# The feed-forward section's last down product in two halves of columns, each summed by VectorE and sent alone

## The reference

```python
x = x + conv_attention(ln_over_channels(x))      # 7x7 windows, softmax, 64 channels
t = to_tokens(x)                                 # (4, 1024, 64)
h = ln_over_channels_of_tokens(t)
for b in range(33):                              # a scan over 33 blocks, 19 kinds each
    op = argmax(h[0, 0, :19])                    # the kind is read from the data
    y = attention(h, wq[b, op], wk[b, op], wv[b, op], wo[b, op])
    h = where(attn_mask[b, op], y, h)
    z = relu(h @ w1[b, op] + b1[b, op]) @ w2[b, op] + b2[b, op]   # 64 -> 256 -> 64
    h = where(ffn_mask[b, op], z, h)
out = t + h
```

## Time and profile before

| what | us |
|---|---|
| median of 3 runs | 239.64 (239.6 to 239.88) |
| the profiled execution's own time | 239.32 |
| its span in the profile | 237.2 |
| first feed-forward section, first product to last store | 93.4 to 109.7 |
| second one, its last store | 232.3 to 233.0 |
| first and last start of an output transfer's issue | 229.2 and 234.4 |

### The profile page before, as it was taken

One profiled execution on the slowest core, in us unless ns is written; L12 is line 12 of the kernel. 1 busy time (PEld: TensorE's weight loads), 2 busy tenths in 40 slices (PEclk: granted clock), 3 DMA queues, 4 the chain that ended last, 5 costly groups with the idle time before them and its releaser, 6 DMA issues.

```text
span 237.2 us, 5409 instructions
## 1 busy us (share of the span) xinstructions
PE 222.1 (94%) x1995; PEld 153.4 (65%) x1996; DVE 158.4 (67%) x294; ACT 156.1 (66%) x304; POOL 26.2 (11%) x37
## 2 busy tenths in 40 slices
PE   7999799999899979999999999999999999998991
PEld 3376477666667665422666778887888888885230
DVE  1387456667757754664869999877779778743642
ACT  2573824767687785554589978699777777773641
POOL 9600321212121006200000000000000000000000
PEclk9999999999999999999999999999999999999999
DMA  5600000000000000001000000000000000000016
GB/s 148 146 3 0 3 6 0 3 0 3 19 15 3 1 3 0 0 4 39 7 3 0 1 3 0 3 1 3 0 3 0 3 0 1 3 3 0 0 34 145
DMA packets 3151, 3.60 MB, mean 15 GB/s; under 512 B 1077, under 2 KB 2229, under 8 KB 3126
## 3 DMA queue, kind: packets, MB, share of 16 engines
q1 hardware_dynamic: 2486, 2.59, 4.6%
q10 hardware_dynamic: 544, 0.66, 1.1%
q0 software_dynamic: 96, 0.00, 0.0%
HBM read 2.21 MB, written 1.05 MB: 14 GB/s over the span
## 4 chain that ended last, share of the span: by engine, by line
PE 77%; ACT 10%; DVE 7%; issue 5%; DVEq 0%; ACTq 0%
PE ps L680 12%; PE ps L666 12%; PE ps L645 12%; PE ps L733 6%; PE ps L747 6%; PE ps L507 4%; PE ps L495 4%; PE ps L469 3%; PE ps L381 2%; DVE negmax L1152 2%; ACT prob L862 2%; PE ps L346 2%; PE ps L425 2%; PE ps L369 2%; PE ps L626 2%
## 5 line engine op out<-in xcount | busy, mean ns | idle before, releaser
L999 ACT COPY arena<-ps 128x1024 f32<-128x1024 f32 x32 | 32.3, 1010 | 16.1 <-PE ps L666 15.9
L645 PE MATMUL ps<-h_st,g_st 128*128 128x512 f32 x128 | 38.7, 424 | 0.7 <-ACT late L947 0.4
L1249 DVE TENSOR_REDUCE negmax<-ps 128x1 f32<-128x1024 f32 x32 | 38.4, 1218 | 1.4 <-PE ps L645 1.3
L947 ACT ACTIVATE late<-ps,negmax 128x1024 f32<-128x1024 f32 x32 | 35.8, 1119 | 4.9 <-DVE negmax L1249 4.4
L666 PE MATMUL ps<-eye,late 128*128 128x128 f32 x256 | 33.5, 274 | 0.6 <-DVE late L1259 0.2
L666 PEld LDWEIGHTS ps<-eye,late 128*128 128x128 f32 x256 | 29.1, 140 | 6.9 <-DVE late L1259 2.7
L680 PE MATMUL ps<-arena,late 128*64 128x128 f32 x512 | 31.5, 276 | 1.1 <-ACT arena L999 1.1
L680 PEld LDWEIGHTS ps<-arena,late 128*64 128x64 f32 x512 | 27.6, 137 | 3.8 <-issue 2.2
L862 ACT ACTIVATE prob<-ps,negmax 128x308 f32<-128x308 f32 x32 | 16.3, 514 | 20.9 <-DVE negmax L1152 20.9
L645 PEld LDWEIGHTS ps<-h_st,g_st 128*128 128x128 f32 x128 | 21.8, 188 | 8.9 <-issue 3.2
L1259 DVE TENSOR_SCALAR late<-late,rinv 128x1024 f32<-128x1024 f32 x32 | 24.1, 754 | 1.1
(11 more groups left out here) (125 smaller groups left out, 314.8 us busy)
## 6 DMA issues: line engine op xcount, KB each, us to landing
out<-osum SPq DMA_DIRECT2D x8, 128.0 KB, 2.4
x<-in_x SPq DMA_DIRECT2D x2, 256.0 KB, 5.2
x<-in_x ACTq DMA_DIRECT2D x2, 256.0 KB, 5.8
onehot<-in_key_onehot SPq DMA_DIRECT2D x2, 133.0 KB, 2.8
w1d<-in_ffn_w SPq DMA_DIRECT2D x4, 64.0 KB, 2.2
w2p<-in_ffn_pack SPq DMA_DIRECT2D x2, 65.5 KB, 1.9
spread_w<-in_spread_mat SPq DMA_DIRECT2D x4, 32.0 KB, 5.5
mean_w<-in_mean_mat SPq DMA_DIRECT2D x1, 96.0 KB, 2.3
```

Source lines behind the costliest of these rows:

```text
L645: mm = nc.tensor.matmul(ps[:, 2 * h + c, :], g_st[:, b2, h, q0:q0 + P], h_st[:, b2, h, part, c * 512:c * 512 + 512], start=(part == 0), st ...
L947: nc.scalar.activation(pr[:, n % 2, :], ps[:, 2 * (n % 2):2 * (n % 2) + 2, :], ACT.Exp, bias=negmax[:, 0, n % 2:n % 2 + 1], accum_out=rows ...
L999: nc.scalar.copy(prt[:, n // 8 % 2, n % 2, :, q0:q0 + P], ps[:, bank:bank + 2, :].rearrange("p b (c q) -> p (b c) q", c=4)).then_inc(S["s_ ...
L1249: nc.vector.tensor_reduce(negmax[:, 0, n % 2:n % 2 + 1], ps[:, 2 * (n % 2):2 * (n % 2) + 2, :], mybir.AxisListType.XY, ALU.max, negate=Tru ...
```

## The change

TensorE's `down(3)` is replaced by `down_halves`: the same terms, but 256 columns at a time, the first half into bank 5 and the second into bank 7 (`LAST_AT`), counting `half_done` after the first and `hid_down` after the second. Both terms wait for all eight ReLUs.

VectorE takes each half from PSUM, adds bias and x in one operation, writes `osum`, and counts `half_summed` and `summed`. It does so after `load_next(1)` where the section is the first, and then waits for the last `h_ready` before it counts `ffn_done`. ScalarE's `store_halves` waits until `summed` has all four chunks of this section, and writes `h2` in two operations of 256 columns. The sync engine issues ten transfers in place of eight: three pairs for the first chunks, a pair of 64 KB transfers for each half of the last. GpSimd and attention's last store count `half_summed` too, so that every way to the end has it.

```diff
+LAST_AT = (5, 7)
...
-            for j in range(4):
+            def put(at, n):
+                for h in range(2):
+                    sp.dma_start(o_parts[at // NPOS][h][:, at % NPOS:at % NPOS + n],
+                                 osum[C * h:C * h + C, at:at + n]).then_inc(S["stored"], 16)
+
+            for j in range(3):
                 sp.wait_ge(S["summed"], base + j + 1)
                 sp.sem_inc(S["passed"], 1)
-                for h in range(2):
-                    sp.dma_start(o_parts[j // 2][h][:, (j % 2) * 512:(j % 2) * 512 + 512],
-                                 osum[C * h:C * h + C, j * 512:j * 512 + 512]).then_inc(S["stored"], 16)
-            sp.wait_ge(S["stored"], 16 * 8)
+                put(j * 512, 512)
+            sp.wait_ge(S["half_summed"], done + 1)
+            sp.sem_inc(S["passed"], 1)
+            put(3 * 512, 256)
+            sp.wait_ge(S["summed"], base + 4)
+            sp.sem_inc(S["passed"], 1)
+            put(3 * 512 + 256, 256)
+            sp.wait_ge(S["stored"], 16 * 10)
...
+                def down_halves():
+
+                    pe.wait_ge(S["relu_act"], 8 * f + 8)
+                    pe.wait_ge(S["relu_dve"], 8 * f + 8)
+                    for half, bank in enumerate(LAST_AT):
+                        for i in range(2):
+                            c = i ^ 1
+                            for h in range(2):
+                                mm = nc.tensor.matmul(ps[C * h:C * h + C, bank, 0:256],
+                                                      w2p[:, c * C:c * C + C],
+                                                      hid[1][:, 2 * h + c, 256 * half:256 * half + 256],
+                                                      start=(i == 0), stop=(i == 1))
+                        mm.then_inc(S["hid_down"] if half else S["half_done"], 1)
...
                 down(2)
-                down(3)
+                down_halves()
...
+                def store_halves():
+                    act.wait_ge(S["summed"], act.snap(4 * act.snap(a + f)) + 8)
+                    for half, bank in enumerate(LAST_AT):
+                        at = 3 * 512 + 256 * half
+                        ins = nc.scalar.activation(h2[:, at:at + 256], ps[:, bank, 0:256],
+                                                   ACT.Identity, bias=w2p[:, 2 * C + 2:2 * C + 3])
+                    ins.then_inc(S["h_ready"], 1)
...
                 if first:
                     load_next(1)
-                store(3)
+                store_halves()
...
                 if first:
                     load_next(1)
+                dve.wait_ge(S["normed_summed"], 4)
+                for half, bank in enumerate(LAST_AT):
+                    at = 3 * 512 + 256 * half
+                    dve.wait_ge(S["hid_down"] if half else S["half_done"], 4 * f + 4 if half else f + 1)
+                    if half:
+                        dve.sem_inc(S["passed"], 1)
+                    nc.vector.scalar_tensor_tensor(
+                        osum[:, at:at + 256], ps[:, bank, 0:256], w2p[:, 2 * C + 2:2 * C + 3],
+                        x2f[:, at:at + 256], ALU.add, ALU.add
+                        ).then_inc(S["summed"] if half else S["half_summed"], 1)
                 dve.wait_ge(S["h_ready"], chunks + 8)
                 dve.sem_inc(S["ffn_done"], 1)
-                add_up(3)
```

More of the change, by code:

```diff
@@ L155, in build @@
             h_ready twice_set twice_ready twice_high twice_low key_high key_twin key_low key_low_twin
-            hid_ready relu_act relu_dve hid_down summed stored""".split()
+            hid_ready relu_act relu_dve hid_down half_done summed half_summed stored""".split()
         S = {n: sem(n) for n in names}
@@ L291, in _ @@
             run(attention, feed_forward)
-            base = sp.snap(4 * sp.snap(sections()))
-            for j in range(4):
+            done = sp.snap(sections())
+            base = sp.snap(4 * done)
+            def put(at, n):
[3 more added lines that the diff above has]
+            for j in range(3):
                 sp.wait_ge(S["summed"], base + j + 1)
                 sp.sem_inc(S["passed"], 1)
-                for h in range(2):
-                    sp.dma_start(o_parts[j // 2][h][:, (j % 2) * 512:(j % 2) * 512 + 512],
-                                 osum[C * h:C * h + C, j * 512:j * 512 + 512]).then_inc(S["stored"], 16)
-            sp.wait_ge(S["stored"], 16 * 8)
+                put(j * 512, 512)
[6 more added lines that the diff above has]
+            sp.wait_ge(S["stored"], 16 * 10)
         @block.gpsimd
@@ L338, in _ @@
             pool.wait_ge(S["normed_summed"], 4)
+            pool.sem_inc(S["half_summed"], 1)
             pool.sem_inc(S["summed"], 4)
@@ L1278, in store @@
                     dve.wait_ge(S["h_ready"], chunks + 5 + g)
+                    if g == 3:
+                        half = slice(g * 512, g * 512 + 256)
+                        s = slice(g * 512 + 256, g * 512 + 512)
+                        nc.vector.tensor_tensor(osum[:, half], h2[:, half], x2f[:, half], ALU.add
+                                                ).then_inc(S["half_summed"], 1)
                     nc.vector.tensor_tensor(osum[:, s], h2[:, s], x2f[:, s], ALU.add).then_inc(S["summed"], 1)
```

## The result

The changed kernel takes 245.07 us (median of 4 runs, 242.29 to 245.4) against 239.62 (238.99 to 239.88): the ratio is 1.021, with a 95% interval of 1.0177 to 1.0243. The forecast was 241.9 with a range to 242.7. The direction was right; the size was more than double, 5.45 us where 2.2 was forecast.

A forecast was written before the change was run, and what follows sets the result against it. TensorE was taken as the bound, holding three quarters of the chain. The terms 1.79 + 0.42 = 2.21 us on the profiled 239.32 gave 241.53, plus 0.32 for the median 241.85, said as 241.9; range 240.9 to 242.7.

The forecast's parts named there:

- TensorE's part: Last down product as eight products of 256 columns in place of four of 512: costs nothing.
- The first run, +1.79: Feed-forward before attention: halves behind `load_next(1)`, stores behind halves; attention's first product at 111.55 in place of 109.76, +1.79 us.
- the line: Straight line between measured 128- and 512-column operations, giving 256-column lengths: 0.42 us on VectorE, 0.49 on ScalarE.
- the rival in which the loads don't hold VectorE: First section: half 0 goes right behind `add_up(2)`, attention starts at 110.39; +1.05 with the end, 240.7 us; chance 0.07.
- The second run, +0.42: Feed-forward after attention: ten output issues start the last 0.74 later, narrower transfer saves 0.32; +0.42 us.
- the rival of cheap narrow issues: Output's end: if a 64 KB issue cost half (0.27), +1.41 in all, 241.05 us; chance 0.12.
- TensorE's clock falls: TensorE idles 2.5 us before attention; at half clock its first two steps cost 2.2 more, 244.1 us; chance 0.04.
- the time outside the span: Whole execution: 2.1 us around the span of 237.2, kept in the profiled 239.32 that the costs were added to.
- the forecast's 2.21: Both sections' costs together, 1.79 + 0.42 = 2.21 us; chance of both costs 0.68.

The follow-up runs named there:

- Experiment 5: Kernel before, with only TensorE's last down product cut into eight products of 256 columns into the same bank: 240.10 us, ratio 1.0017.
- experiment 2: Changed kernel with VectorE's `load_next(1)` moved behind the two half sums: 241.87 us, ratio 1.0091.
- experiment 3: Changed kernel with halves only in the feed-forward section behind attention, the first section as in the kernel before: 239.85 us, ratio 1.0013.
- experiment 4: Changed kernel with the last chunk's two halves sent together, eight transfers of 128 KB: 242.09 us, ratio 1.0115.
- experiment 7: Kernel before, with VectorE summing the whole last chunk straight from PSUM ahead of ScalarE's store, second section only: 239.14 us, ratio 0.9977.
- experiment 9: Kernel before, with three copies on ScalarE delaying its last store in the first section, nothing else of the change: 242.70 us, ratio 1.0116.
- experiment 10: Kernel before, with three ScalarE copies delaying the first section's last store and four filler products on TensorE in the gap: 241.26 us, ratio 1.0067.
- experiment 11: Changed kernel with four filler products on TensorE ahead of attention's wait for the last `h_ready`, measured again: 242.38 us, ratio 1.0123.
- experiment 12: Changed kernel unedited, run again on another chip, beside its version with fillers: 244.20 us, ratio 1.0187 against the kernel before.
- experiment 1: Changed kernel with four filler products on TensorE after attention's folding products, ahead of its wait for the last `h_ready`: 242.39 us, ratio 1.0133.
- experiment 6: Changed kernel's half products, but ScalarE stores each half first, VectorE adds from SBUF behind it, last chunk sent whole: 239.53 us, ratio 0.9996.
- experiment 8: Changed kernel unedited, run again on another chip: 243.78 us, ratio 1.0174 against the kernel before.

## Why the prediction was wrong

- **TensorE's part** (nothing): right. Experiment 5 can't be told from the kernel before, the distance of the stores is 1.73 against 1.72.
- **The first run, +1.79**: right. The mechanism (halves behind the register loads, stores behind the halves) is in the trace step by step, 1.66 us by the first product's place, 1.77 when the 0.11 by which this execution was ahead at `store(2)` (107.19 against 107.30) is counted. That it fits within 0.02 is in part luck, as the terms erred against each other: the halves started at 109.62 where 109.84 was forecast, VectorE's half lasts 480 ns where the line gave 420, the pair 0.88 for 0.76; ScalarE's pair 0.84 for 0.87. Of the rival in which the loads don't hold VectorE nothing was seen; with the loads moved behind, experiment 2, about half the cost goes.
- **The second run, +0.42**: right, 0.39 in the trace, by 0.74 of more issues and a landing of 2.0 in place of 2.4. A 64 KB issue lasts as long as a 128 KB one, so the rival of cheap narrow issues is out. Experiments 3, 4 and 7 show the same bound from three sides.
- **The step that failed: the rival "TensorE's clock falls", ruled out with a chance of 0.04 and left out of the range.** I read the earlier trace rows as saying that a gap of 2.5 us is safe, since 1.00 was granted for over 3.2 us after the last product. One row at full clock shows that the clock can stay, not that it must. In the changed kernel it fell 1.6 us after the last folding product, and those are small: from 108 us to the fall TensorE was busy for 1.33 us. The row was also of the kernel's end, where no product follows whose length would show a fall. Experiments 9 to 12, on one chip, are the proof: the gap alone brings the fall (5 of 6 executions, 6 of 6 in the changed kernel), and fillers in it take the fall away at the same lateness (none of 8, one of 6). It costs 2.86 us in the profiled execution, and 1.4 to 1.8 in the medians with and without fillers. That rival's price, 2.2, was the right order, though the clock stayed at half for a third step too; its chance wasn't. The page "TensorE: Matmul & The Clock Gate" of the Trainium skill, part 1, has the clock follow recent activity. The traces agree, down to the fillers.
- **A term that wasn't in the sum**: the time outside the span, taken as fixed at 2.1 us. It is 3.1 in the profiled execution. In each of the profiles in which the trace has an instruction fetch behind the end (the changed kernel's first and third, experiments 2, 4, 5 and 10), 3.1 to 3.4 us lie outside; in the others (experiments 1, 3, 6, 7, 8, 9, 11) 1.9 to 2.1. Experiments 8 and 12 are one program with both, so an execution of one program can go either way. Whether it can at all goes with the code: the table above has it in 26 of 76 executions with a longer TensorE program and in none of 75 without, and experiment 5 lengthens nothing else. That the execution waits for the fetch is argued from this list, not shown by an edit, and why it comes in some executions only is open.

With full clock the forecast's number would have lain in its range, but not by its sum. The two executions of the changed kernel without a fall took 242.29 and 242.40: their spans, 239.2 and 239.3, are 2.0 and 2.1 above the profiled 237.2, a little under the forecast's 2.21, and their time outside is 3.1 us, 1 us more than the forecast had. The medians with fillers, 242.38 and 242.39, have their additional time in the output's issues instead.

## What to carry to other kernels

When an edit makes TensorE wait longer, price the clock as well as the wait: here 1.7 us more of waiting cost up to 2.9 more behind it, in 14 of 16 executions. Four products on idle data in the gap took most of that away. And ask what a shared routine does in each place where it is called: work put ahead of a store for the sake of the last section also ran in the first, behind 1.5 us of register loads and ahead of everything in attention. Sending earlier is worth nothing when the queue that issues is busy; the gain, 0.5 us, was in one whole sum straight from PSUM, in the last section alone. And look at the span and at the time outside it in every execution, not in the profiled one alone: an edit that only made TensorE's program longer changed the second in 3 of 10.

## What the runs showed of the hardware

- TensorE's clock went to half in or right behind a gap of 2.0 to 2.1 us in the three traces of the changed kernel, and of 1.95 us in experiment 9's; the mean clock has a fall in 14 of 16 executions and 5 of 6. In the kernel before this gap is 0.3 us and the clock 1.00. By the clock rows it stayed at half for 6.8 us in the first (0.96 + 2 + 2 + 1.88) and for 3.4 in the last (0.24 + 2 + 1.16).
- An output issue on the sync queue lasts 0.47 to 0.60 us at 64 KB and at 128 KB, but 1.43 and 1.64 us while a 16 KB block of instructions was fetched (experiments 1 and 11). That the fetch is the cause is argued from these two.
- A fetch of instructions behind the last landing goes with 1.0 to 1.3 us more outside the span (six profiles, 3.1 to 3.4 against 1.9 to 2.1). Over 2.3 us outside were seen only in kernels whose TensorE program is longer than before, in 26 of 76 executions.
